# Batch 0's first scores get their maxima by selecting matmuls; x's second turn is read by VectorE

## The reference

```
xn = layer_norm(x, norm_w, norm_b)
q = (xn @ q_w + q_b)   k = (xn @ k_w + k_b)          # 16 heads of 16
att[n, m, h] = q[n, h] . k[m, h] + (1 - mask[n]) * -1000000.0
att = softmax(att, axis=2)                           # over m
v = (xn @ v_w + v_b) * mask
y = einsum('bnmh,bmhl->bnhl', att, v)
scale, shift = split(silu(cond) @ emb_w + emb_b)
out = x + silu(layer_norm(y, sb_norm_w, sb_norm_b) * (1 + scale) + shift) @ out_w + out_b
```

## Time and profile before

| | |
|---|---|
| median of 3 runs | 531.52 us (530.69 to 532.24) |
| the profiled execution | 530.54 us, its span 528.8 us |
| busy | PE 96%, DVE 79%, ACT 67%, POOL 43% |
| TensorE's granted clock | 1.00 throughout |
| chain that ended last | PE 80%, DVE 8%, POOL 3%, ACT 2% |

### The profile page before, as it was taken

The page is one execution under the profiler, slowest core; times in us unless marked ns, Lnnn a source line. Parts: engine busy times, 40 slices in busy tenths (PEclk is TensorE's granted clock), DMA queues, the critical chain, the costliest instruction groups (busy, mean ns, idle before and its releaser), DMA issues.

```text
span 528.8 us, 10102 instructions
## 1 busy us (share of the span) xinstructions
PE 505.5 (96%) x2848; PEld 189.1 (36%) x2851; DVE 417.3 (79%) x661; ACT 355.0 (67%) x645; POOL 227.6 (43%) x270
## 2 busy tenths in 40 slices
PE   8898999999999999999999999999999999998986
PEld 3422333434333333333334333334333333332334
DVE  6796778787897879797897879888797978888525
ACT  2316766777867777777857788576867778666761
POOL 4385214535444534535434544436335543334011
PEclk9999999999999999999999999999999999999999
DMA  5445353333423543234423543235433443233021
GB/s 153 121 122 171 94 171 100 101 88 115 124 80 111 153 142 101 82 103 141 123 78 117 150 138 93 76 101 145 131 89 120 122 121 91 81 109 103 22 59 40
DMA packets 55098, 57.95 MB, mean 110 GB/s; under 512 B 12424, under 2 KB 42248, under 8 KB 55072
## 3 DMA queue, kind: packets, MB, share of 16 engines
q1 hardware_dynamic: 52464, 55.40, 35.9%
q10 hardware_dynamic: 2608, 2.24, 1.4%
HBM read 36.35 MB, written 21.00 MB: 108 GB/s over the span
## 4 chain that ended last, share of the span: by engine, by line
PE 80%; DVE 8%; issue 4%; POOL 3%; ACT 2%; DMA 1%; DVEq 0%; POOLq 0%; SPq 0%; ACTq 0%
PE pv_ps L577 22%; PE st_ps L561 21%; PE mx_ps L525 11%; PE job_ps L625 8%; PE job_ps L634 5%; PE job_ps L646 4%; DVE negmax L932 4%; PE mx_ps L671 3%; DVE h_t L1012 2%; PE mx_ps L538 1%; ACT probs L725 1%; PE mx_ps L605 1%; PE mx_ps L679 1%; DMA k_rows<-qk_dram 1%; PE job_ps L491 1%
## 5 line engine op out<-in xcount | busy, mean ns | idle before, releaser
L932 DVE TENSOR_REDUCE negmax<-mx_ps 128x2 f32<-128x1024 f32 x256 | 304.2, 1219 | 82.2 <-PE mx_ps L525 81.3
L725 ACT ACTIVATE probs<-st_ps 128x512 f32<-128x512 f32 x502 | 272.2, 595 | 123.3 <-PE st_ps L561 122.7
L561 PE MATMUL st_ps<-q_rows,k_rows 115*128 115x512 bf16 x502 | 154.9, 383 | 2.7 <-ACT probs L725 2.3
L577 PE MATMUL pv_ps<-probs,v_rows 128*32 128x512 f32 x1024 | 136.4, 605 | 0.6 <-ACT probs L725 0.6
L1210 POOL TENSOR_TENSOR qk_parts<-qk_rest,qk_parts 128x512 bf16<-128x512 f32 x31 | 36.0, 1162 | 135.8 <-DVE qk_parts L1006 135.8
L525 PE MATMUL mx_ps<-k_rows,q_rows 51*128 51x512 bf16 x512 | 78.9, 382 | 1.8 <-DMA k_rows<-qk_dram 1.8
L561 PEld LDWEIGHTS st_ps<-q_rows,k_rows 115*128 115x128 bf16 x502 | 39.3, 98 | 102.8 <-ACT probs L725 69.4
L1195 POOL TENSOR_TENSOR qk_parts<-qk_full,zero 128x512 bf16<-128x512 f32 x29 | 31.2, 1076 | 77.3 <-ACT qk_full L747 77.3
L625 PE MATMUL job_ps<-x_norm_t,w_qk 128*128 128x512 f32 x116 | 59.5, 593 | 0.0
L525 PEld LDWEIGHTS mx_ps<-k_rows,q_rows 51*128 51x128 bf16 x512 | 15.7, 94 | 110.0 <-DVE negmax L932 52.5
L1201 POOL TENSOR_TENSOR qk_rest<-qk_full,qk_parts 128x512 f32<-128x512 f32 x31 | 37.2, 1199 | 4.3 <-ACT qk_parts L739 2.0
(11 more groups left out here) (116 smaller groups left out, 395.1 us busy)
## 6 DMA issues: line engine op xcount, KB each, us to landing
qk_dram<-qk_parts SPq DMA_DIRECT2D x128, 128.0 KB
q_rows<-qk_dram SPq DMA_DIRECT2D x124, 96.0 KB, 2.6
k_rows<-qk_dram SPq DMA_DIRECT2D x124, 96.0 KB, 2.6
x_in<-in_x SPq DMA_DIRECT2D x16, 256.0 KB, 3.0
x_res<-in_x SPq DMA_DIRECT2D x8, 512.0 KB, 4.3
out<-out_sb SPq DMA_DIRECT2D x16, 256.0 KB, 2.5
k_rows<-mask_dram SPq DMA_DIRECT2D x64, 6.0 KB
w_e<-in_L_cond_emb_w ACTq DMA_DIRECT2D x4, 256.0 KB, 3.0
```

Source lines behind the costliest of these rows:

```text
L561: pe.matmul(st_bank(b, t, h), k_rows[0:ROWS_ALL, g, h, c * P:(c + 1) * P], q_rows[0:ROWS_ALL, g, h, :], start=True, stop=True).then_inc(st ...
L577: mm = pe.matmul(pv_ps[VW * h:VW * (h + 1), :], v_rows[:, c, g * GH + h, :], probs[:, t % P_SLOTS, h, :], start=(c == 0), stop=(c == CH - ...
L725: act.activation(probs[:, t % P_SLOTS, h, :], st_bank(b, t, h), ACT.Exp).then_inc(exp_done, 1)
L932: dve.tensor_reduce(by_pair[:, :, j, c], mx_ps[j][:, :, :], AXIS_X, ALU.max, negate=True).then_inc(max_done, 1)
```

## The change

In the prologue, POOL clears v_rows and builds `select` (16 x 16 x 128, bf16: for each of 16 rows a matrix that picks this row for all 128 keys) right after its chunk of x, ahead of its presets. DVE reads x's second turn itself, between two steps of mask_rows. ACT writes part 0 of group 0 right from the bank, without qk_full; DVE computes the rest from the same bank. k_rows' second memset comes behind silu. Part 1 of group 1 is cast by ACT. SP copies q_rows of group 0, whose max rows are still zero, to q_first. The scores of step 0 are computed from q_first, and eight small matmuls per head add the maxima into the same bank. They stand in the prologue's last two steps. In steps 0 to 4 of batch 0 the maxima stand in another order, and the two x turns are jobs instead of side jobs. Fewer warm-up matmuls are left.

```diff
+JOBS_0 = {**JOBS, 1: ("xturn", 0, 1, AZ), 2: ("xturn", 1, 1, AZ)}
+SIDE_0 = {t: of for t, of in SIDE.items() if of[0] != "xturn"}
+FIRST_MAX = {0: ((0, 0),), 1: ((0, 1), (1, 0)), 2: ((1, 1),), 3: ((2, 0), (2, 1), (3, 0)), 4: ((3, 1), (4, 0), (4, 1))}
-LATE_FIRST = {(11, 0): ("proj", 1, 1), (14, 1): ("proj", 2, 1)}
+LATE_FIRST = {(14, 1): ("proj", 2, 1)}
-WARM_FIRST = {2: 5, 8: 4}
+WARM_FIRST = {2: 3, 8: 4}
 WARM_MAX = {(0, 0): 3, (0, 1): 3, (1, 0): 3, (1, 1): 3, (2, 0): 3, (2, 1): 3, (3, 0): 3, (3, 1): 6,
-            (4, 0): 3, (4, 1): 3, (5, 0): 3, (6, 0): 3}
+            (4, 0): 3}
...
+            def first_score(h):
+                if h == 0:
+                    pe.wait_ge(first_filled, 16)
+                    pe.wait_ge(rest_filled[0], REST_DMAS * 16)
+                    pe.wait_ge(select_ready, 1)
+                    pe.wait_ge(max_split, 1)
+                    pe.wait_ge(cond_ready, 1)
+                    pe.wait_ge(part0_ready, NG - 1)
+                wait(pe, exp_done, h - ST_BANKS + 1)
+                ps = st_bank(0, 0, h)
+                pe.matmul(ps, k_rows[0:ROWS_ALL, 0, h, 0:P], q_first[0:ROWS_ALL, h, :], start=True, stop=True)
+                for c in range(CH):
+                    for part in range(2):
+                        mm = pe.matmul(ps[:, c * P:(c + 1) * P], select[:, h * CH + c, :], max_parts[:, 0, part, :],
+                                       start=False, stop=True, skip_group_check=True)
+                mm.then_inc(st_ready, 1)
...
+            def first_steps(t):
+                if t > 0:
+                    st_unit(0, t, 0)
+                    st_unit(0, t, 1)
+                    pv_step(0, t)
+                for lead, j in FIRST_MAX[t][0:2]:
+                    max_pair(0, lead, j)
+                if t > 0:
+                    st_unit(0, t, 2)
+                    st_unit(0, t, 3)
+                for lead, j in FIRST_MAX[t][2:]:
+                    max_pair(0, lead, j)
+                job(t, 0)
+                max_turn(0, t)
+            def last_lead(t):
+                if t == STEPS - 2:
+                    max_turn(-1, t)
+                    max_quad(-1, t)
+                    first_score(0)
+                    first_score(1)
+                else:
+                    max_pair(-1, t, 0)
+                    first_score(2)
+                    first_score(3)
+                    max_pair(-1, t, 1)
+                    job(t, -1)
...
+                if kind == "proj" and in_prologue(d, i) and i == 0:
+                    if half == 0:
+                        act.wait_ge(turned["proj"], 1)
+                        act.activation(qk_parts[:, 0, :], ps, ACT.Identity, bias=qkb_col[:, 0:1]).then_inc(part0_ready, 1)
...
+                    if in_prologue(d, i) and i == 2:
+                        act.wait_ge(rest_ready, 2)
+                        act.wait_ge(copies_saved, 16 * PARTS)
+                        act.copy(qk_parts[:, 1, :], qk_rest[:, :]).then_inc(part1_ready, 1)
...
                 dve.tensor_copy(mask_parts[:, 0, :], mask_bias[:, :]).then_inc(setup_chain, 1)
+                dve.wait_ge(norm_loaded, 2 * 16)
+                dve.wait_ge(turned["xturn"], KD)
+                dve.tensor_scalar(x_norm_t[:, 1, :], mx_ps[0][:, 0, :], nw_col[:, 1:2], nb_col[:, 1:2],
+                                  ALU.mult, ALU.add).then_inc(xt_ready, 1)
...
                 dve.wait_ge(part0_ready, 1)
-                dve.tensor_tensor(qk_rest[:, :], qk_full[:, :], qk_parts[:, 0, :], ALU.subtract).then_inc(rest_ready, 1)
+                dve.wait_ge(qk_loaded, QK_DMAS * 16)
+                dve.scalar_tensor_tensor(qk_rest[:, :], mx_ps[0][:, 1, :], qkb_col[:, 0:1], qk_parts[:, 0, :],
+                                         ALU.add, ALU.subtract).then_inc(rest_ready, 1)
...
                     mask_rows()
-                    dve.memset(k_rows[0:HALF + P // 4, NG // 2:NG, :, :].bitcast(F32), TWO_ONES).then_inc(k_preset, 1)
                     first_parts()
                     silu_of_cond()
+                    dve.memset(k_rows[0:HALF + P // 4, NG // 2:NG, :, :].bitcast(F32), TWO_ONES).then_inc(k_preset, 1)
...
                     x_norms(0, 1)
+                    preset_v()
+                    pool.tensor_copy(select[:, :, :], ident[0:GH * CH, 0:GH * CH].unsqueeze(2).broadcast_to(
+                        (GH * CH, GH * CH, P))).then_inc(select_ready, 1)
                     presets()
...
+                    if first and i == 1:
+                        sp.wait_ge(own_filled[0], OWN_DMAS * 16)
+                        sp.wait_ge(rest_filled[0], REST_DMAS * 16)
+                        sp.dma_start(q_first[0:ROWS_ALL, :, :], q_rows[0:ROWS_ALL, 0, :, :]).then_inc(first_filled, 16)
                     save(3, 2, part2_ready)
```

More of the change, by code:

```diff
@@ L128, in work_at, with of_loop @@
     return (kind, i, b + db) + table[step][3:]
-def of_loop(b, first, middle, last):
+def of_loop(b, first, middle, last, second=None):
+    if second is not None and isinstance(b, int) and b == 0:
+        return second
     return first if isinstance(b, int) and b == -1 else last if isinstance(b, int) and b == B - 1 else middle
@@ L144, in job_at @@
         b, step = b - 1, step + STEPS
-    return work_at(of_loop(b, FIRST_JOBS, JOBS, LAST_JOBS), b, step)
+    return work_at(of_loop(b, FIRST_JOBS, JOBS, LAST_JOBS, JOBS_0), b, step)
 def side_at(b, step):
@@ L151, in side_at @@
         b, step = b - 1, step + STEPS
-    return work_at(of_loop(b, {}, SIDE, LAST_SIDE), b, step)
+    return work_at(of_loop(b, {}, SIDE, LAST_SIDE, SIDE_0), b, step)
 def late_at(b, step, place):
@@ L251, in attention_layer @@
         k_rows = sb("k_rows", [P, NG, GH, T], BF16)
+        q_first = sb("q_first", [P, GH, T], BF16)
+        select = sb("select", [GH * CH, GH * CH, P], BF16)
         negmax = sb("negmax", [P, 2, GH * CH])
@@ L295, in attention_layer @@
         max_filled = [sem(f"max_filled{i}") for i in range(NG)]
+        first_filled = sem("first_filled")
         out_saved = sem("out_saved")
+        select_ready = sem("select_ready")
         warm_ready = sem("warm_ready")
@@ L367, in emptied @@
             if kind == "proj":
-                return full_ready, NG * batch + i + 1
+                return full_ready, NG * batch + i
             if kind == "yturn":
@@ L495, in max_quad, with max_pair @@
             def max_quad(b, t):
+                for j in range(PAIRS):
+                    max_pair(b, t, j)
+            def max_pair(b, t, j):
                 ahead = t + MAX_LEAD
@@ L504, in max_quad @@
                 first = isinstance(mb, int) and mb == 0
[L505 to L512, removed]
-                        pe.wait_ge(part0_ready, j + 1)
[L515 to L530, removed]
@@ new lines, in max_pair @@
+                if first and step == 0:
+                    if j == 0:
+                        pe.wait_ge(xt_ready, KD)
+                        pe.wait_ge(rest_ready, 1)
+                        pe.wait_ge(cond_ready, 1)
+                    else:
+                        pe.wait_ge(v_plain_ready, 1)
+                        pe.wait_ge(part0_ready, j + 1)
+                wait(pe, max_done, PAIRS * (STEPS * mb + step - 1) + j + 1)
+                if j == 0 and side_at(b, t - 1):
+                    wait(pe, *emptied(*side_at(b, t - 1)))
@@ new lines, in max_pair @@
+                if j == 1 and turn_at(b, t):
+                    turn, turn_b = turn_at(b, t)
+                    pe.wait_ge(max_split, NG * turn_b + turn + 1)
+                for half in range(2):
+                    base, h = HALF * half, PAIRS * half + j
+                    pe.matmul(mx_ps[j][:, half, :], q_rows[base:base + ROWS_MX, g, h, c * P:(c + 1) * P],
+                              k_rows[base:base + ROWS_MX, g, h, :], start=True, stop=True,
+                              tile_position=(base, 0)).then_inc(max_ready, 1)
@@ new lines, in max_pair @@
+                if first:
+                    keep_warm(pv_ps, WARM_MAX.get((step, j), 0))
+            def first_score(h):
[4 more added lines that the diff above has]
+                    pe.wait_ge(max_split, 1)
+                    pe.wait_ge(cond_ready, 1)
+                    pe.wait_ge(part0_ready, NG - 1)
[7 more added lines that the diff above has]
+                mm.then_inc(st_ready, 1)
@@ L543, in st_unit @@
                 g, c = t // CH, t % CH
-                if c == 0 and h == 0:
+                first = isinstance(b, int) and b == 0 and g == 0
+                if c == (1 if first else 0) and h == 0:
                     pe.wait_ge(rest_filled[g], REST_DMAS * 16 * (b + 1))
                     pe.wait_ge(max_filled[g], 2 * 16 * (b + 1))
-                    if isinstance(b, int) and b == 0 and g == 0:
-                        pe.wait_ge(cond_ready, 1)
-                        pe.wait_ge(part0_ready, NG - 1)
                 u = GH * t + h
@@ L680, in side @@
                 mm.then_inc(turned[kind], 1)
+            def first_steps(t):
```

(25 more changed lines are left out.)

7 lines of the change are left out of this document (4 added, 3 removed).

## The result

The changed kernel takes 540.46 us in the median of four runs (535.23 to 541.47), the kernel before 531.88 beside it: a ratio of 1.0133, 95% interval 1.0068 to 1.0198. It is slower by 8.6 us; I had forecast 532.1 and a range to 534.4. The profiled execution is the fastest of the four, 535.23 us, and its span of 533.5 shows only part of the loss. With two more, six executions are on record, in two groups: 535.1 and 535.2 us with a mean granted clock of 0.996, and 539.8 to 541.5 us with 0.987 to 0.990.

The account below looks back on a forecast made before the run. TensorE, busy 96% of the span, was taken as the bound, so the start of batch 0's step 5 counts. Opening +2.1 and lower part -1.5 gave +0.6 us: 532.1 us on the median, range 528.6 to 534.4.

Parts of the forecast that it names:

- Opening, in the way: Opening: POOL's new memset and select copy stop DVE instructions; DVE's split at 16.72 instead of 14.59, +2.1 us.
- the third step: Opening: DVE's third x_norm step, expected behind POOL's memset, so x's last chunk is normalised at 10.6 instead of 8.89.
- Opening, meant to go: Opening: DVE reads x's second turn beside ACT (-0.4), ACT's qk_full leaves the path (-0.65); sum -1.05 us.
- The first max pair: End of the opening's chain: DVE's first pair of maxima forecast to start at 25.4, against 23.27 before.
- DVE's free 2.5 us: Opening: DVE free 2.5 us before the first maximum, so k_rows' second memset of 1.76 us counted as hidden.
- I price it at nothing: Lower part: q_first's extra DMA on SP's queue, ahead of one save, priced at no cost; uncovered, about 0.6 us.
- 0.7 to spare: Lower part: the landing of group 1's fills was taken to have some 0.7 us of slack.
- a rival's tail: Rival C, opening: slow select copy and PE cools down; +2.0 us by the copy, +4 with the clock, about 534; chance 0.20.
- Lower part: From DVE's split to step 5: earlier first scores and a cast moved to ACT; step 5 at 55.45 instead of 56.99, -1.5 us.
- my order: Lower part: PE's sequence laid out by hand from 33.85 through steps 1 to 4, with step 5 starting at 55.45.
- the sign that I had named for no gain: Lower part: if step 5 still follows the first max pair by 33.7 us (32.2 forecast), it gave nothing.
- the 0.09 priced: Lower part: time in us of one 128-column selecting matmul, between bounds 0.06 and 0.11; a head takes 0.96 us.

Follow-up runs that it names:

- e4_before_pool: Kernel before, with POOL clearing v_rows and building an unused select copy right behind its x_norm; 534.08 us, ratio 1.0050.
- g1_open: Kernel before with the opening's edits alone: no select copy, first scores or q_first, old order of steps, POOL as before; 530.48 us, ratio 0.9987.
- f1_noq: Changed kernel without q_first and its DMA; first scores read q_rows, group 0's max rows are placed behind the fourth score; 534.64 us, ratio 1.006.
- f3_before_q: Kernel before plus q_first's DMA, unread, at the changed kernel's place in SP's queue; group 0's max rows wait for it; 537.58 us, ratio 1.0104.
- h1_q_one: Kernel before plus q_first's DMA, unread, copying one head of four (115 KB instead of 460); 532.51 us, ratio 1.0015 to the kernel before.
- e3_warm: Changed kernel with 12 instead of 4 warm-up matmuls behind the turn of the condition; 539.13 us, ratio 1.0135 to the kernel before.
- e1_port: Changed kernel, but POOL builds select behind part 2 of group 0 and clears v_rows at its old place; 538.9 us, ratio 1.0142 to the kernel before.
- f4_noq_port_order: Changed kernel without q_first, POOL's select built later and v_rows cleared as before, old order in steps 0 to 4 of batch 0; 531.95 us, 0.9996.
- g2_before_wm: Kernel before with WARM_MASK 6 instead of 12, so fewer warm-up matmuls; 531.57 us, ratio 1.0003.

## Why the prediction was wrong

**Opening, in the way: right.** Forecast were the projection at 14.1 and the split at 16.7; they came at 14.00 and 16.72, and e4_before_pool shows the mechanism alone, +2.2 us. The port's rule from the Trainium skill ("SBUF — State Buffer", "Who interferes with whom") holds in its first half, that the lock is for a whole instruction: the step of 7.99 ended at 10.31, the memset at 10.16. In its second half, that the first to issue wins, it does not hold here: the normalising step of 7.99 had been waiting when the memset began at 8.36, and the memset went first. (At 18.40 in the kernel before it was the waiting VectorE instruction that went first.) I had the memset hold up the third step, it held up the second; and the select copy held up mask_bias, not the cast. That the sum came out all the same is luck: each of the two blocks fell on another instruction of the same chain. The copy took 1.88; I had priced 2.1, where my own rows give 1.95 (0.19 + 2044 x 0.86 ns).

**Opening, meant to go: nearly right.** -1.05 was priced for it, and 0.95 us arrived in g1_open.

**The first max pair, forecast at 25.4: 26.09.** I had called k_rows' second memset hidden under DVE's free 2.5 us, and then laid POOL's blocks over the same time without adding them up. x_vareps took 1.13 us beside POOL's qk_rest (0.16 before), and cond_t came last. In f1_noq, with the same opening, the fill came last, and the pair at 25.22.

**"I price it at nothing": the step that failed.** I looked at q_first as an issue in SP's queue (0.6 us, 0.7 to spare), and not as 460 KB in front of group 1's own fills. Those ended PE's wait at 33.56 in the kernel before, in its trace, so nothing could be put in front of them for free: the "0.7 us to spare" was not there. The DMA costs 5.6 us alone (f3_before_q), a quarter of its bytes 0.9, not told from nothing (h1_q_one), and taking it away gives back 5.8 of the 8.4 us by which the forecast missed (f1_noq). In the profiled execution of 535.23 us little of this is seen, a wait of 0.22 us. In e3_warm's of 541.42 it is 2.1 us of wait and 5.8 of half clock behind it.

**The clock: seen only as a rival's tail.** I tied it to the idle time in front of the first projection, under a slow select copy. The copy was not slow, and the clock fell elsewhere, behind idle time at 24 us or at pair 8; no rival had that. In the changed kernel the executions at a mean clock of 0.987 to 0.990 take 5 to 6 us more than those at 0.996. No trace of them is kept. Their nearest relatives, e1_port and e3_warm at 0.987, spend 29.9 and 29.8 us from pair 8 to step 5 instead of 24.1, so I take the difference to be the half clock there.

**Lower part, -1.5 us: mis-sized.** From the turn of the maxima to step 5 my order gave 22.6 us (32.9 to 55.45). Without q_first it is 24.6, and in the profiled execution of the changed kernel also (37.08 to 61.66). From the first max pair to step 5 it takes 35.6 us there and 33.8 in f1_noq; 33.7 was the sign that I had named for no gain. The selecting matmuls were not at fault, they took 0.55 us for eight in the chain, 0.07 each, less than the 0.09 priced. That is also less than the 81 ns that the Trainium skill gives ("TensorE: Matmul & The Clock Gate", "Back-to-back issue gap"). Steps 3 and 4 took 4.6 us each where I had 4.05 and 3.8, 1.4 of the 2.0: a third pair waits for DVE's maximum of the first, and the half projection behind it takes 1.05 and not 0.86. The old order avoids that, and still gains nothing (f4_noq_port_order, 24.0). My reading, not tested, is that the scores leave PE's stretch earlier, but 2.2 us of selecting matmuls and the chain of maxima fill it again.

## What to carry to other kernels

A DMA added off the critical path is priced by its bytes against the next transfer that somebody waits for, not by its issue: 460 KB ahead of a fill of 96 KB made that fill 3.7 us late. Where the next such transfer already ends a wait, there is nothing to spare. A memset or copy on GpSimd placed in an idle gap of its own engine isn't free if VectorE runs copies, casts or tensor_scalars from SBUF to SBUF at that time; look at those in the trace for durations above their fastest. And where a change makes the matmul engine wait longer, price the clock behind the wait too: here it added 2.0 us in one kernel and 5.8 in another. A wait that is shortened early may only come back later, in front of the next transfer, and cost more there (e1_port, e3_warm).

## What the runs showed that I had not expected

GpSimd's next instruction overtook a VectorE instruction that had been waiting for 0.4 us. The same twelve warm-up matmuls ran at full rate in the traces of some kernels (2.76 us) and at about half of it in others (4.24 to 4.87). The row of the changed kernel:

```profile
6.38 4.87 PE L472 MATMUL pv_ps<-warm_in 128*128 128x512 bf16 x12
```

The granted clock of that stretch reads 1.00 all the same. h1_q_one, otherwise the kernel before but for its small DMA, had them slow in its profiled execution (4.68 us), and there the first max pair came at 25.32 instead of 23.27; so they can cost 2 us, though g2_before_wm, with six of them, spreads as widely as the kernel before. Eight matmuls of 128 columns with 16 rows, each with its own weights, take 0.55 us in the chain; in the list of single instructions each stands with 0.214 us, because they overlap.
